# Two-layer graph network: query products in three bfloat16 parts, work moved off VectorE in the edge attention, weights and rows loaded at other times

## The reference, cut to what matters

```
q = (xn @ Wq + bq).reshape(n, H, DH)          # likewise k, v
ep = ef @ We + be                             # edge features, one row of 32 per edge
scores = einsum('ehd,ehd->eh', q[dst], k[src] + ep[:, None, :]) * scale * ew[:, None]
m = segment_max(scores, dst)
ex = exp(scores - m[dst])
s = segment_sum(ex, dst)
out = segment_sum((ex / s[dst])[:, :, None] * v[src], dst)
```

```
logits = mean(x) @ Wr + br
top_w, top_i = top_k(softmax(softmax(logits) * scale), 2)
y_e = gelu(x @ W1[e] + b1[e]) @ W2[e] + b2[e]
```

## Time and profile before

| what | value |
|---|---|
| runs of the kernel before | 3642.98 us median of 3 (3642.55 to 3644.26) |
| the profiled execution | 3640.97 us, its span 3639.0 us |
| instructions | 50484 |
| PE / DVE / ACT / POOL busy, share of the span | 83% / 58% / 47% / 53% |
| mean granted PE clock | 0.887 |

### The profile page before, as it was taken

How to read it: one execution, slowest core, us unless ns; L and a number is a source line. 1 busy time by engine, 2 the same in 40 slices (tenths; PEclk the granted TensorE clock), 3 DMA queues, 4 the chain that set the end, 5 groups by cost and what they waited for, 6 DMA issues and landing times. The chain is left out here.

```text
span 3639.0 us, 50484 instructions
## 1 busy us (share of the span) xinstructions
PE 3021.7 (83%) x12620; PEld 2281.7 (63%) x12620; DVE 2119.2 (58%) x4741; ACT 1716.8 (47%) x3980; POOL 1923.4 (53%) x1876
## 2 busy tenths in 40 slices
PE   2778677778778599779849999999999999889798
PEld 2556555555555588656437777777777777656565
DVE  6333334333334500175559999999999999843415
ACT  2434333333333322233246666667666666542323
POOL 3777777777773344301036666666666666530010
PEclk9777767887868599989769999999999999889899
DMA  6555555555551256641057777777777777510001
GB/s 162 147 146 149 140 156 140 156 141 147 143 146 34 68 197 219 185 160 59 9 182 221 219 215 223 210 219 221 218 216 222 218 214 224 154 67 0 27 0 36
DMA packets 354070, 547.21 MB, mean 150 GB/s; under 512 B 172814, under 2 KB 224275, under 8 KB 353509
## 3 DMA queue, kind: packets, MB, share of 16 engines
q0 software_dynamic: 113216, 348.74, 33.1%
q1 hardware_dynamic: 232710, 183.43, 17.0%
q10 hardware_dynamic: 7887, 12.08, 1.0%
HBM read 493.34 MB, written 51.90 MB: 150 GB/s over the span
## 5 line engine op out<-in xcount | busy, mean ns | idle before, releaser
L2989 POOL DMA_INDIRECT store<-kv_d,src_of x832 | 869.5, 1045 | 422.5 <-issue 245.7
L859 POOL DMA_INDIRECT agg_rows<-xn_d,src_of x832 | 791.5, 951 | 268.4 <-issue 243.1
L1031 PE MATMUL agg_sums<-agg_rows,agg_member 128*128 128x257 f32 x1664 | 582.8, 497 | 255.2 <-DVE acc L923 132.8
L872 ACT ACTIVATE agg_rows<-agg_rows,weight_of 128x256 f32<-128x256 f32 x832 | 375.2, 500 | 614.6 <-DMA agg_rows<-xn_d,src_of 611.7
L1031 PEld LDWEIGHTS agg_sums<-agg_rows,agg_member 128*128 128x128 f32 x1664 | 374.4, 245 | 415.2 <-DVE acc L923 185.2
L923 DVE TENSOR_TENSOR acc<-acc,agg_sums 128x257 f32 x416 | 176.3, 424 | 580.6 <-PE agg_sums L1031 566.1
L3021 PE MATMUL flash_query<-q,flash_mem_t 128*128 x1664 | 412.7, 392 | 50.6 <-DVE store L3226 38.8
L3034 PE MATMUL flash_sums<-store,flash_member 128*128 128x264 f32 x1664 | 424.8, 388 | 2.2 <-DVE store L3291 2.2
L3021 PEld LDWEIGHTS flash_query<-q,flash_mem_t 128*128 128x128 f32 x1664 | 312.7, 193 | 103.7 <-issue 57.4
L3034 PEld LDWEIGHTS flash_sums<-store,flash_member 128*128 128x128 f32 x1664 | 318.4, 191 | 56.8 <-issue 2.2
L3144 ACT ACTIVATE acc<-flash_sums 128x264 f32 x416 | 159.2, 383 | 254.5 <-PE flash_sums L3041 254.5
(11 more groups left out here) (483 smaller groups left out, 4597.6 us busy)
## 6 DMA issues: line engine op xcount, KB each, us to landing
moe_w<-in_L_ffn_W_dram SPq DMA_DIRECT2D x64, 512.0 KB, 4.5
agg_feats<-in_ef_t_dram SPq DMA_DIRECT2D x208, 128.0 KB
flash_goal<-goal_d SPq DMA_DIRECT2D x52, 512.0 KB, 4.3
agg_rows<-xn_d,src_of POOLq DMA_INDIRECT x832, 2.8
ep_d<-agg_ep SPq DMA_DIRECT2D x52, 256.0 KB
store<-kv_d,src_of POOLq DMA_INDIRECT x832, 4.1
flash_ep<-ep_d SPq DMA_DIRECT2D x416, 32.0 KB
flash_flags<-flags_d SPq DMA_DIRECT2D x416, 32.0 KB
```

What stands on the lines that cost most here:

```text
L859: pool.indirect_dma_start(rows[:, q, 0:D], None, sh.xn_d, bass.IndirectOffsetOnAxis(ap=sh.src_of[:, c:c + 1], axis=0)).then_inc(gathered[u ...
L872: act.activation(rows[:, q, 0:D], rows[:, q, 0:D], ACT.Copy, scale=sh.weight_of[:, bass.ds((UI * i + u) * SUBS + k, 1)]).then_inc(weighted, 1)
L1031: last = pe.matmul(sums[:, j % 4, 0:W], member[:, c % (2 * BI * SUBS), :], rows[:, c % NB, :], start=(c % SUBS == 0), stop=(c % SUBS == SU ...
L2989: pool.indirect_dma_start(ring[:, s, :], None, sh.kv_d, bass.IndirectOffsetOnAxis(ap=sh.src_of[:, c:c + 1], axis=0)).then_inc(gathered[p][ ...
```

## The change

1. **Query in three bfloat16 parts.** `stage_mid` splits `q` into a high, a middle and a low part (ACT and DVE, 7 steps of four tiles among the 14 blocks); `ask` makes three bfloat16 products where it made one in float32. The space for the low part comes from keeping `sh.work` in memory (`work_d`): stored at the end of `stage_mid`, read and written tile by tile in `stage_flash`, and read back whole at its end.
2. **Chain operations.** `first_hot` is a table column loaded by DMA; `diag` and the copy of `run` are made by ACT; the two `z` become one instruction; the mask `bar` is added by a product on PE; the subtraction `low` becomes a second product that accumulates on PE.
3. **Order.** `reduce(s, 0)` stands behind `mult(s, 0)`, before `rescale`.
4. **Waits.** SP's `flags` load waits for `back_ready` and not for `p_ready`; `scale` waits for `back_ready` of the window before.
5. **Weights.** The routing weights load in `stage_attention_out`. The experts' weights load in `stage_route` as soon as the two numbers are known, and `stage_ffx` waits for the up and the down weights apart.

```diff
 # stage_mid, ACT, from block 7 on; DVE does rest and lowest from block 6 on
+                def parts(n):
+                    a, e = SPLIT[n]
+                    act.wait_ge(rest_ready, n + 1)
+                    act.activation(sh.q_parts[:, a:e, 0:D], sh.q_parts[:, a:e, 1::2], ACT.Copy).then_inc(high_kept, 1)
+                    act.wait_ge(high_kept, n + 1)
+                    act.activation(sh.q_parts[:, a:e, D:2 * D], rest_of(n), ACT.Copy).then_inc(middle_kept, 1)
...
+                    dve.tensor_tensor(rest_of(n), sh.q[:, a:e, :], sh.q_parts[:, a:e, 1::2], ALU.subtract
+                                      ).then_inc(rest_ready, 1)
...
+                    dve.tensor_tensor(sh.q_low[:, a:e, :], rest_of(n), sh.q_parts[:, a:e, D:2 * D], ALU.subtract
+                                      ).then_inc(low_kept, 1)
...
 # stage_mid, SP
+                    sp.wait_ge(rows_done, e)
+                    sp.dma_start(sh.work_d[:, a:e, :], sh.work[:, a:e, :]).then_inc(sh.work_out[n], 16)
...
 # stage_flash, SP
+                for n in range(used):
+                    sp.wait_ge(sh.work_out[n], 16)
+                sp.dma_start(w2_s, w2).then_inc(weights_in, 16)
...
-                        sp.wait_ge(p_ready, w - 1)
+                        sp.wait_ge(back_ready, w - 1)
...
+                def work_load(i):
+                    if i >= 3:
+                        sp.wait_ge(work_stored[i % 3], 16 * (i // 3))
+                    sp.dma_start(work[:, i % 3, :], sh.work_d[:, i, :]).then_inc(work_in[i % 3], 16)
...
+                    if i >= 2:
+                        work_store(i - 2)
+                    if i + 1 < NT:
+                        work_load(i + 1)
...
+                sp.dma_start(sh.work[:, :, :], sh.work_d).then_inc(sh.work_back, 16)
...
 # stage_flash, PE
-                            last = pe.matmul(query[:, c * D:(c + 1) * D], mem_t[:, g % 2, c * P:(c + 1) * P],
-                                             sh.q[:, bass.ds(t, 1), :], start=True, stop=True)
+                            to, hot = query[:, c * D:(c + 1) * D], mem_t[:, g % 2, c * P:(c + 1) * P]
+                            pe.matmul(to, hot, sh.q_parts[:, bass.ds(t, 1), 0:D], start=True, stop=False)
+                            pe.matmul(to, hot, sh.q_parts[:, bass.ds(t, 1), D:2 * D], start=False, stop=False)
+                            last = pe.matmul(to, hot, sh.q_low[:, bass.ds(t, 1), :], start=False, stop=True)
...
+                        pe.matmul(carried, sh.ident[:, :], bar[:, :, :].rearrange("p a j -> p (a j)"), start=True, stop=False)
...
-                        pe.transpose(pt[:, 0:P], low[:, :], sh.ident[:, :])
+                        pe.wait_ge(diag_ready, a.at + 1)
+                        pe.matmul(pt[:, 0:P], sh.ident[:, :], scaled[:, :], start=True, stop=False)
+                        pe.matmul(pt[:, 0:P], top, minus[:, :], start=False, stop=True)
...
 # stage_flash, ACT
+                        act.wait_ge(chain_ready, a.at + 1)
+                        act.activation(diag[:, :], sh.ident[0:H, 0:H], ACT.Copy, scale=fall[:, 0:1]).then_inc(diag_ready, 1)
+                        act.activation(run[:, 0:1], run[:, WS:WS + 1], ACT.Copy)
...
 # stage_flash, DVE
-                    dve.tensor_scalar(z[:, 0, :], own[:, :], ahead[:, P - 1:P], None, ALU.mult)
-                    dve.drain()
-                    dve.tensor_scalar(z[:, 1, :], own[:, :], top[:, 0:1], None, ALU.mult).then_inc(z_ready, 1)
+                    dve.drain()
+                    dve.tensor_tensor(z[:, :, :], own[:, :].unsqueeze(1).to_broadcast([P, 2, WS]),
+                                      outer.unsqueeze(2).to_broadcast([P, 2, WS]), ALU.mult).then_inc(z_ready, 1)
...
-                    dve.tensor_scalar(first_hot[:, :], sh.lane[0:H, :], steps[:, a.side, 4 * WS:4 * WS + 1], None, ALU.is_equal)
...
-                    dve.tensor_scalar(diag[:, :], sh.ident[0:H, 0:H], fall[:, 0:1], None, ALU.mult)
-                    dve.tensor_copy(run[:, 0:1], run[:, WS:WS + 1])
...
-                    dve.tensor_tensor(picked[:, :, :], carried.rearrange("p (a j) -> p a j", a=2),
-                                      bar[:, :].unsqueeze(1).to_broadcast([P, 2, WS]), ALU.add)
-                    dve.drain()
...
-                        dve.drain()
-                    dve.tensor_tensor(low[:, :], st, top[:, :], ALU.subtract).then_inc(p_ready, 1)
+                    last.then_inc(p_ready, 1)
...
                         mult(s, 0)
+                        reduce(s, 0)
...
-                        reduce(s, 0)
                         reduce(s, 1)
...
 # stage_route, SP
+                sp.wait_ge(expert_ready, 1)
+                e = [sp.value_load(sh.expert[0:1, q:q + 1], min_val=0, max_val=7) for q in range(2)]
+                for q in range(2):
+                    for to, of in up_of(q, e[q]):
+                        sp.dma_start(to, of).then_inc(sh.ffx_up_in[q], 16)
+                    sp.dma_start(*down_of(q, e[q])).then_inc(sh.ffx_down_in[q], 16)
```

More of the change, by code:

```diff
@@ L2024, in stage_ffx @@
         down = ctx.enter_context(nc.psum_tensor("ffx_down", [P, GT, 512], F32))
-        weights_in = [sem(f"weights_in{q}") for q in range(2)]
         affine_in = sem("affine_in")
@@ L2172, in stage_mid @@
     LEAD = 2
+    SPLIT = [(a, min(a + 4, NT)) for a in range(0, NT, 4)]
     with ExitStack() as ctx:
@@ L2272, in stage_mid, with rest_of @@
         xt_stored = sem("xt_stored")
+        rest_ready = sem("rest_ready")
+        high_kept = sem("high_kept")
+        middle_kept = sem("middle_kept")
+        low_kept = sem("low_kept")
+        rows_done = sem("rows_done")
+        def rest_of(n):
+            a, e = SPLIT[n]
+            return nr[:, n % 2 * 4:n % 2 * 4 + e - a, :]
         def block_of(q):
@@ L2571, in _ @@
                         exp(q - 1)
+                    if 7 <= q < 7 + len(SPLIT):
+                        parts(q - 7)
                 exp(NB - 1)
+                act.wait_ge(low_kept, len(SPLIT))
                 def third_norms(g):
@@ L2764, in _ @@
                     feature(q - 1)
+                    rest(q - 6)
+                    if q >= 7:
+                        lowest(q - 7)
                 dve.wait_ge(pe_small, 3)
@@ L2769, in _ @@
                     feature(q - 1)
+                    if q - 6 < len(SPLIT):
+                        rest(q - 6)
+                    lowest(q - 7)
                 feature(NB - 1)
@@ L2840, in stage_flash @@
         bo_s = sh.store[:, 2 * WS * KV + KB * 2 * F1:2 * WS * KV + KB * 2 * F1 + D]
-        w2_s = sb("w2", [P, 2 * FB, D])
+        spare = sh.work[:, :, :].rearrange("p t f -> p (t f)")
+        W2_AT, HIDDEN_AT, XT_AT, END = 3 * D, 3 * D + 2 * FB * D, 3 * D + 2 * FB * D + FB * P, 3 * D + 2 * FB * D + FB * P + KB * P
+        used = sum(a * D < END for a, e in BACK)
+        work = spare[:, 0:3 * D].rearrange("p (q f) -> p q f", q=3)
+        w2_s = spare[:, W2_AT:HIDDEN_AT].rearrange("p (m f) -> p m f", m=2 * FB)
+        hidden = spare[:, HIDDEN_AT:XT_AT].rearrange("p (m n) -> p m n", m=FB)
+        xt_s = spare[:, XT_AT:END].rearrange("p (k n) -> p k n", k=KB)
         b1_s = sb("b1", [P, 2 * FB])
-        xt_s = sb("xt", [P, KB, P])
-        hidden = sb("hidden", [P, FB, P])
         goal = sb("goal", [P, 2, WS * P], BF16)
-        mem_t = sb("mem_t", [P, 2, 512])
+        mem_t = sb("mem_t", [P, 2, 512], BF16)
         member = sb("member", [P, 2, 4, P])
@@ L2870, in stage_flash @@
         diag = sb("diag", [H, H])
-        first_hot = sb("first_hot", [H, P])
+        minus = sb("minus", [P, P])
         pa = sb("pa", [P, P + H])
@@ L2914, in stage_flash @@
         down_added = sem("down_added")
+        diag_ready = sem("diag_ready")
+        work_in = [sem(f"work_in{q}") for q in range(3)]
+        work_stored = [sem(f"work_stored{q}") for q in range(3)]
         def tile_numbers(eng, w):
@@ L3204, in _ @@
                 dve.drain()
-                dve.tensor_scalar(bar[:, :], own[:, :], row_j[:, 0:1], -4.0 * BIG, ALU.not_equal, ALU.mult)
+                for n in range(2):
+                    dve.tensor_scalar(bar[:, n, :], own[:, :], row_j[:, 0:1], -4.0 * BIG, ALU.not_equal, ALU.mult)
                 dve.tensor_scalar(row_head[:, :], own[:, 0:H], sides[:, 0:1], None, ALU.is_equal)
@@ L3802, in build, with up_of, down_of @@
         sh.b2_row = sb("b2_row", [P, D])
-        stage_route(nc, sh, blocks(a["L1_ffn_Wr"]), a["L1_ffn_br"], a["L1_ffn_b2"])
-        def expert1(array, pattern):
-            def part(q):
-                e = nc.sync.value_load(sh.expert[0:1, q:q + 1], min_val=0, max_val=7)
-                return a[array][bass.ds(e, 1)].rearrange(pattern, p=P)
-            return part
-        stage_ffx(nc, sh, expert1("L1_ffn_W1", "e (k p) f -> p (e k) f"), expert1("L1_ffn_W2", "e (k p) f -> p (e k) f"),
-                  expert1("L1_ffn_b1_f", "e p k -> p (e k)"), a["L1_ffn_gamma"], a["L1_ffn_beta"], out)
+        sh.ffx_w1 = sb("ffx_w1", [P, 2, KB, F1])
```

(11 more changed lines are left out.)

130 lines of the change are left out of this document (84 added, 46 removed).

## The result

The changed kernel takes 3618.46 us (median of 4, 3612.64 to 3619.54) against 3643.62 for the kernel before on the same chip: a ratio of 0.9925, with a 95% interval of 0.9908 to 0.9942: 0.75% faster, clear of the noise. The forecast was 3607. The profiled execution took 3612.64 us with a span of 3610.9, 28.1 less than before, of the forecast 35.6. It is the quickest of the four; the medians lie 25.2 apart, so about 3 of the 28.1 may be chance.

The account below looks back on a forecast made before the run. It took the edge attention's chain through PE and DVE as the bound, neither engine alone. Passes -36, stage ends +2, middle stage +4, routing and experts -5.6 make -35.6 us: forecast 3607, own range 3585 to 3627.

Parts of the forecast that it names:

- The chain: Edge attention, DVE: operations moved off save 1.05 us per pass; scaling to product of quad 0 takes 6.1 to 6.3.
- The later sums: Edge attention, PE: sums start 4.1 us after product of quad 0, idle 1.0; DVE waits 1.0; pass +0.36.
- The bfloat16 query: Edge attention, PE: three bfloat16 parts take 1.28 us per quad, saving 0.45, mostly not on the path.
- the passes' term: Edge attention: pass falls from 24.65 to 23.96 us; -36 us over 50 passes and two more at the ends.
- I take 0 in the loop: Edge attention, SP's queue and DMAs: added residual-row traffic costs 0 in the loop, 10 us as upper end.
- its bounds: Term ranges: passes -15 to -85 us, stage ends 0 to 6, middle 0 to 8, routing -3 to -7.5.
- The middle stage: Middle stage: splitting q makes ACT's block 3.6 us against 2.92; the divisor comes 4 us later (0 to 8).
- Routing and experts: Routing weights loaded before give -2.5 us; with earlier expert loads, together -5.6 us (-3 to -7.5).
- A: Edge attention: DVE never waits; passes 23.0 us, -85 instead of -36, total 3558 us; chance 0.09.
- C: Edge attention, PE: bfloat16 weight loads not hidden, a quad costs 2.8 us, total 3682 us; chance 0.04.
- D: Gain eaten: PE's late transpose and later sums take 0.6 per pass, split costs 8; total 3641 us; chance 0.11.
- B: Edge attention: the clock falls in every pass, each of 50 loses 1.9 us, total 3702 us; chance 0.07.

Follow-up runs that it names:

- e10: Changed kernel with the query products in float32 again and no split of q: 3642.76 us, ratio 0.9989 to the kernel before.
- e11: Changed kernel with the queries of quads 2 and 3 one step sooner on PE and ACT: 3706.51 us, ratio 1.0155 to the kernel before.
- e1: Changed kernel without the residual rows' reads and writes in the edge attention's loop: 4486.9 us, ratio 1.0416 to the kernel before.
- e2: Changed kernel with 12 gathers per window instead of 16 after the second window: 4221.26 us, ratio 0.9789 to the kernel before.
- e8: Changed kernel with the first quad's column sums back in their old place: 4451.87 us, ratio 1.0362 to the kernel before.
- e3: Same kernel as e11, on a chip where the kernel before took 4273 to 4326 us: 4424.22 us, ratio 1.0273.
- e4: Kernel of e3 with 12 gathers per window instead of 16 after the second window: 4281.75 us, ratio 0.9946 to the kernel before.

## Why the prediction was right, and where its size was off

The direction, the mechanism and most terms held on the chips like that of the kernel before.

- **The chain.** Scaling to product of quad 0 was to take 6.1 to 6.3 us. It took 6.60 and 6.27, of which 0.62 and 0.24 are the waits for rows; without them 5.98 and 6.03, so the stretch gave 1.25 a pass and not 1.05. From the ends to the product it is 3.24 (forecast 3.4).
- **The later sums.** 4.13 after the product of quad 0 (4.1), idle 1.08 (1.0), product to product 10.82 and 10.76 (10.68), DVE's wait 1.05 (1.0). The rescaling waits for nothing, as said. I predicted that the moved reduction pays for that with the later sums; e10 shows the bill in full, when the query isn't shorter.
- **The bfloat16 query.** 1.31 us per quad, taken as 1.28. The estimate by the formula of the Trainium skill ("TensorE: Matmul & The Clock Gate", Back-to-back issue gap) was 1.31, and the trace agrees with it (2522.61 to 2523.92 for twelve); it is 0.03 a pass away from the term that the sum used.
- **The step that failed** is the size of the passes' term, -36 for 52 passes with "I take 0 in the loop" for the DMAs. A pass without late rows is now 10.79 + 7.07 + 6.00 = 23.86, 0.79 below 24.65 and better than my 0.69; 51 of them would give -40. What it doesn't give is lost to irregular passes: beyond such clean passes, and the 3.4 by which the last one was longer before, the 51 passes spend 21.4 us after against 6.5 before. In every pass over 24.45 us but the first the long stretch is the one in which DVE waits for gathered rows; it waits 29.1 us for them in the whole stage, 4.5 of it at one addition of the last pass (3129.24), where the 3.2 MB of residual rows are read back (issued at 3116.17, landed at 3128.9). I had read POOL's 67% and the DMAs' 0.74 as room. But POOL waited for PE's sums in every pass, and that idle time went: 151.9 us over 1950 to 3080 became 72.6, or 3.3 us per 16 gathers became 1.6. Only 0.5 of the 1.8 is the shorter pass; 1.2 is that the gathers themselves take longer, 1124 ns in the mean instead of 1048 in that window: not more of them are long (154 over 1.2 us against 170), but those that meet a weighing of DVE take 1.46 us in the mean instead of 1.18 (last section). Their landing went from 4.1 to 5.2 us. That the traffic of the residual rows is not the cause by itself, e10 supports (same traffic, pass of 24.9, gathers of 1067 ns, 1.8 us of late rows), and that POOL's room is what counts, e11 too (places freed later and longer gathers, 106 us); the test made for it (e1, e2) met 4300 chips, so the 15 us are read from the trace and not shown by removing them.
- **What offset it.** The clean pass (some 4 us in all) and the routing (1.75) gave more than forecast. Without these the time would have been some 6 us longer; that it still lies near the forecast is in part their doing. The forecast's own range, 3585 to 3627, does not come out of its bounds: added up they reach from about 3550 to 3649.
- **The middle stage.** +3.9 at the divisor (4). The blocks are 3.1 to 3.6 us apart and not 3.6, but the split also runs on behind the last long block.
- **Routing and experts.** -7.35 against -5.6: the weights 2.5 as said; SP issues the first load 1.68 us after the expert numbers stand instead of 4.94, and the first product comes 4.18 after that load instead of 5.84.

Of the rivals, A did not happen; e11, which takes DVE's wait away by another order on PE, is slower for what that order costs elsewhere. C is excluded by 1.31 us per quad. D's two reasons did not come (the chain's savings stand, the split costs 3.9), though late rows cost 15. B's clock stays at 1.00 in the loop on this chip. On the 4300 chips the clock is lower behind the holds: in e8 it is 1.00 from 3019 to 3021.8, PE then stands idle for 9.78 us, and from 3031.5 to 3036 it is 0.50. The low clock follows the held signals there, and adds to their cost: the mask's product takes 0.63 us (L3144, 3031.59) where it takes 0.31 at 1.00 (2511.68 in the changed kernel). What no rival named is that the sign may depend on the chip: every variant with a bfloat16 query and all gathers is 2.7% to 4.2% slower than the kernel before on the 4300 chips.

## What to carry to other kernels

When a chain through two engines gets shorter, look at who sleeps in it: the idle time of a third engine that refills a ring (here POOL with its gathers) is the room that the shorter pass will use up, and that engine's own operations may take longer in the new order as well. Taking operations off one engine may pay only if the engine that answers also gets quicker at that place; e10 had the moved work and the new order without the quicker answer and gained nothing that can be told from none. And time a change on more than one chip before trusting a gain below one per cent.

## What the runs showed of the hardware that was not expected

**Signals held during a series of gathers.** On three of the six chips of the experiments TensorE's signals reached DVE and ACT up to 11 us late, and came 2 us after POOL's series of indirect DMAs had ended; the kernel before was 18% slower there. With four gathers fewer and nothing else changed (e3, e4) the longest hold fell by 5.3 us and the time by 142. What differs in these chips, no run here tells.

**Gathers stretched by DVE.** A gather takes 0.94 or 0.95 us on POOL, or up to 2.0 in the changed kernel and 3.0 in e11. POOL and DVE in the changed kernel:

```profile
2516.11 0.94 POOL L3060 DMA_INDIRECT store<-kv_d,src_of  x1 [0.30 <-issue]
2517.36 2.03 POOL L3060 DMA_INDIRECT store<-kv_d,src_of  x1 [0.30 <-issue]
```

The second lies across DVE's second weighing (2516.09 + 2.48 for two), which reads both its inputs from SBUF. Sorted by what DVE did 0.9 us after a gather's start, over 1950 to 3080: of 164 gathers under the product L3308, whose second input is in PSUM, none took over 1.2 us (mean 0.95); of 70 under the weighing L3370 two thirds did (mean 1.66), of 147 under the addition L3301 41% (mean 1.30). The Trainium skill ("SBUF — State Buffer", SBUF: two separate sides) says that DVE and GpSimd share a port pair that one of them locks for a whole instruction, DVE also "with two SBUF inputs (only against a GpSimd op that reads SBUF)". The rows agree with it. The column sums L3312 have one input and yet a quarter of the gathers sorted under them is long (mean 1.08); but each of these also met a weighing or an addition in its first 0.95 us. Sorted that way, 434 of the 745 gathers met one of the two, 154 of them took over 1.2 us, and of the 311 that met neither (141 of them under column sums) none did. The kernel before shows the same: all 170 long gathers met one.
